# Where the last group's gathers stand on GpSimd's queue: behind the first key stack's ones, ahead of the queries' parting and the other fills

## The chip, the cores and the metric

The kernel runs on one core of one Trainium2 chip. Its metric is the device time of one execution in microseconds, the median of several runs; three runs of the kernel before gave 740.69, 741.37 and 742.08 us. The engines are called by these names: TensorE (PE, and PEld for its weight loads), VectorE (DVE), ScalarE (ACT), GpSimd (POOL), and SyncE (SP), which only issues transfers. ScalarE and GpSimd issue transfers too.

## The reference

Two layers over 16 batches of 112 tokens with 256 features, and a context of 375 rows for each batch. Cut to what matters:

```python
x = x + L0_xattn(layernorm(x), ctx, mask)       # one head, softmax over 375 keys, output normalized
# L0_ffn: top 2 of 8 experts, each token's two expert rows weighted and added
weights, indices = top_k(softmax(xh @ gate_w + gate_b), 2)
routed = sum(weights[..., None] * take_along_axis(out_of_experts, indices))
x = x + shared_experts(xh) + routed
# L1_xattn: 16 heads of 16 features, no mask
q, k, v = split_heads(layernorm(x) @ Wq.T), split_heads(ctx @ Wk.T), split_heads(ctx @ Wv.T)
x = x + merge(softmax(q @ k.T * 0.25) @ v) @ Wo.T
x = x + layernorm(x) @ W.T + b + (layernorm(x) @ V_r) @ C.T
```

## The kernel before

Five streams of instructions, one per engine, are written out by hand and meet at semaphores: `wait_ge(s[name], value)` holds an engine, `then_inc` counts up. Each engine works strictly in its own order. Nothing is scheduled by a program; where a call stands in the function of an engine is where it runs.

The tokens are treated in four groups of four batches (`NG = 4`, `G = 4`). The expert stage works through 35 tiles of 128 routed rows. Each tile's result `y` is written to the array `yscr` in device memory by GpSimd (L1480, semaphores `y_out0` and `y_out1`). When all tiles that hold rows of a group are written, `gather` (L1840 to L1848) fetches for each batch j of the group the two expert rows of every token: two indirect transfers of 112 rows by 256 floats into `yg[:, j, k, :]`, `i` being the group. It first waits for `y_out0` and `y_out1`, and for `mixed`, which says that VectorE has combined the former content of the buffer. Groups 0 to 2 are gathered within the expert stage, four transfers in a row, twice each (`gpsimd_beside`). Group 3 needs the last tile, and so its eight gathers stand in the second layer (`gpsimd`, L1863 on). Their rows are scaled by ScalarE beside batches 2 and 3 (`scaled`, L2155) and added by GpSimd (`combine`).

The second layer begins with a prelude, in which TensorE projects the last six contexts to values (`late_values`, L2283), group 2's queries (L2238), and the scores of batches 0 and 1 (`scores`, L2309). The latter are only for the maxima of each head (L1966, VectorE). A batch's maxima are split into three bf16 parts (`parted`, L1754 to L1766, by VectorE for batches 0 and 1, by GpSimd from batch 2 on), turned by TensorE (`maxima_T`, L2314), copied by VectorE (L1972) and laid into the query stack `qst` by three small transfers on SP (`maxima`, L1787, semaphore `mrow_in`). Then follow 16 batches b. In each TensorE computes the transposed scores in four quads of heads and three chunks of keys (`transposed`, L2329), ScalarE takes the exponential (L2166, semaphore `p_ready`), TensorE multiplies with the values (L2338), and beside that computes the scores of batch b + 2.

The fills on GpSimd, and who needs them: `ones_below(b)` (L1731) writes the lower 32 rows of key stack b, which TensorE needs in batch b; the column of ones in `va` (L1875) is needed from batch 10 on; `zeros_below(1)` (L1735) is needed before SP lays batch 4's maxima into the second query stack. `split_queries` and `split_rest` (L1738 to L1752) part group 2's queries into three bf16 parts in four steps; their end, `q3_ready`, releases ScalarE's store of them (L2089), which stands on ScalarE's stream ahead of batch 0's exponentials.

Of the kernel before, what the change touches and what calls it, by code (L numbers as in the profile page):

```python
# [19 lines left out]
NKC = K // KC  # L20
KP = (NKC - 1) * KC + P
C = D // P
G = 4
NG = B // G
# [1593 lines left out]
def second_layer(nc, tensors, first, routed, dram, out, x_res, weight1, weight2, slots, mhalf, ps, bank, ident, new_semaphore, pool_semaphore):  # L1618
# [9 lines left out]
    s = {n: new_semaphore("d_" + n) for n in (  # L1628
        "weights_in", "wf_ps", "wf_ready", "identb_ready", "below_ready", "scaled", "added", "mixed", "xh_ready",
        "q_ps", "q1_ready", "q2_ready", "q3_ready", "q_out", "qs_in0", "qs_in1",  # L1630
        "k_in0", "k_in1", "k_in2", "k_in3", "v_in0", "v_in1", "s_ps", "s_max", "m_ready", "mT_ps", "mT_ready", "clear", "ones_ready",
        "mrow_in0", "mrow_in1", "st_ps", "p_ready", "pv_ps", "outT_ready", "out_ps", "heads_ready", "o_ps", "x3_ready", "bf_added",
        "f_ps", "fl_ps", "bl_added", "res_ready", "res_out")}
# [13 lines left out]
    EARLY = NG - 1  # L1647
# [82 lines left out]
    def ones_below(pool, b):  # L1730
        pool.memset(kst[b][DEPTH:P, :, :].rearrange("p h t -> p (h t)").bitcast(F32), TWO_MINUS_ONES).then_inc(s["ones_ready"], 1)  # L1731
        pool.wait_ge(s["ones_ready"], b + 1)

    def zeros_below(pool, slot):
        pool.memset(qst[slot][DEPTH:P, :, :].rearrange("p h t -> p (h t)").bitcast(F32), 0.0).then_inc(s["below_ready"], 1)  # L1735
        pool.wait_ge(s["below_ready"], slot + 1)

    def split_queries(eng, i):  # L1738

        eng.wait_ge(s["q1_ready"], (i + 1) * C)  # L1740
        if i:
            eng.wait_ge(s["q_out"], i * 16)
        eng.tensor_copy(qa[:, 1, :, :], qr[:]).then_inc(s["q2_ready"], 1)
        eng.wait_ge(s["q2_ready"], 3 * i + 1)
        eng.tensor_tensor(qr[:], qr[:], qa[:, 1, :, :], ALU.subtract).then_inc(s["q2_ready"], 1)

    def split_rest(eng, i):
        eng.wait_ge(s["q2_ready"], 3 * i + 2)
        eng.tensor_copy(qa[:, 2, :, :], qr[:]).then_inc(s["q2_ready"], 1)
        eng.wait_ge(s["q2_ready"], 3 * i + 3)  # L1750
        eng.tensor_tensor(qa[:, 0, :, :], qr[:], qa[:, 2, :, :], ALU.subtract).then_inc(s["q3_ready"], 1)
        eng.wait_ge(s["q3_ready"], i + 1)  # L1752

    def parted(eng, b):  # L1754

        base, slot = b * 4, b % 2
        eng.wait_ge(s["s_max"], b * 8 + 8)
        if b >= 2:
            eng.wait_ge(s["mT_ps"], b - 1)
        eng.tensor_copy(mparts[:, slot, 0, :], mxh[:, slot, :]).then_inc(s["m_ready"], 1)  # L1760
        eng.wait_ge(s["m_ready"], base + 1)
        eng.tensor_tensor(mr[:, slot, :], mxh[:, slot, :], mparts[:, slot, 0, :], ALU.subtract).then_inc(s["m_ready"], 1)
        eng.wait_ge(s["m_ready"], base + 2)
        eng.tensor_copy(mparts[:, slot, 1, :], mr[:, slot, :]).then_inc(s["m_ready"], 1)
        eng.wait_ge(s["m_ready"], base + 3)
        eng.tensor_tensor(mparts[:, slot, 2, :], mr[:, slot, :], mparts[:, slot, 1, :], ALU.subtract).then_inc(s["m_ready"], 1)  # L1766
# [60 lines left out]
    def rstd_of(pool, n, norm, js=slice(0, G)):  # L1827
        pool.wait_ge(s["mv_ready"], MV + norm + 1)
        pool.tensor_scalar(rstd[:, js], mv[:, js, 1], EPS, None, ALU.add).then_inc(s["pool"], 1)
        pool.wait_ge(s["pool"], n())  # L1830
        pool.tensor_tensor(rstd[:, js], rstd[:, js], mhalf[:, js], ALU.pow).then_inc(s["rstd_ready"], 1)

    def normalized_beside(pool, i, norm):

        pool.wait_ge(s["rstd_ready"], MV + norm + 1)
        for j in range(G):
            pool.tensor_scalar(xh[:, j, :], x_res[:, i * G + j, :], mv[:, j, 0:1], rstd[:, j:j + 1],
                               ALU.subtract, ALU.mult).then_inc(s["xh_ready"], 1)

    def gather(pool, i, j):  # L1840
        b = i * G + j
        for q in range(2):
            pool.wait_ge(routed[f"y_out{q}"], (DONE[i] + 1 - q) // 2 * 16)
        if i:
            pool.wait_ge(s["mixed"], 2 * (b - G + 1))
        for k in range(2):
            pool.indirect_dma_start(out=yg[:, j, k, :], out_offset=None, in_=yscr[0:DONE[i] * P, :],  # L1847
                                    in_offset=bass.IndirectOffsetOnAxis(ap=slots[0:S, k, b:b + 1], axis=0)).then_inc(s[f"y_in{j}"], 16)  # L1848
# [13 lines left out]
    def gpsimd(pool, n):  # L1862

        def combine(i, js):
            for j in js:
                for k in range(2):
                    pool.wait_ge(s["scaled"], 2 * j + k + 1)
                    if k:
                        pool.wait_ge(s["added"], 2 * j + k)
                    pool.tensor_tensor(x_res[:, i * G + j, :], x_res[:, i * G + j, :], yg[:, j, k, :], ALU.add).then_inc(s["added"], 1)  # L1870

        ones_below(pool, 1)
        ones_below(pool, 2)
        ones_below(pool, 3)
        pool.memset(va[:, :, :, :, HD:HD + 1], 1.0).then_inc(s["va_ready"], 1)  # L1875
        pool.wait_ge(s["va_ready"], 2)
        zeros_below(pool, 1)
        pool.wait_ge(s["m_ready"], 4)
        split_queries(pool, EARLY - 1)
        split_rest(pool, EARLY - 1)  # L1880
        i = NG - 1
        for j in range(G):
            if j % 2:
                parted(pool, j // 2 + 2)
            pool.wait_ge(s["p_ready"], (2 * j + 2) * NKC)
            gather(pool, i, j)
        for j in range(0, G, 2):
            combine(i, range(j, j + 2))
            parted(pool, j // 2 + 4)
        rstd_of(pool, n, NORMS["q", i])  # L1890
        normalized_beside(pool, i, NORMS["q", i])
        parted(pool, 6)
        parted(pool, 7)
        split_queries(pool, i)
        split_rest(pool, i)
        for i, batches in enumerate(((8,), (9, 10, 11, 12), (13, 14, 15))):
            for b in batches:
                parted(pool, b)
            rstd_of(pool, n, NORMS["f", i])
            normalized_beside(pool, i, NORMS["f", i])  # L1900
            add_bias(pool, i)
        i = NG - 1
        rstd_of(pool, n, NORMS["f", i], AHEAD)
        rstd_of(pool, n, NORMS["f", i] + 1, LAST)
# [360 lines left out]
    def tensor(t):  # L2265
# [219 lines left out]
        def project_one(i, j):  # L2485
# [46 lines left out]
        project_part("f", LAST, wf)  # L2532

    return {"sync": sync, "gpsimd": gpsimd, "vector": vector, "scalar": scalar, "tensor": tensor, "gpsimd_beside": gpsimd_beside,
            "vector_beside": vector_beside, "scalar_beside": scalar_beside, "tensor_beside": tensor_beside}

# [128 lines left out]
```

## Time and profile before

| what | value |
|---|---|
| median of three runs | 741.37 us (740.69 to 742.08) |
| profiled execution, its own time | 743.03 us |
| its span, first to last instruction | 741.2 us |
| TensorE busy | 721.4 us, 97% of the span |
| VectorE, ScalarE, GpSimd busy | 470.0, 309.8, 271.5 us |
| mean granted clock of TensorE | 0.995 |
| first and last gather of group 3 issued | 552.1 and 570.2 us |
| prelude of the second layer, batches 0 to 3 | 520 to 545 us, 545 to about 590 us |

Shares of busy time are averages over the span, and TensorE's busy time is modelled from the starts of its matmuls, so a full TensorE row doesn't say that it never waited. An engine's idle time matters only where it stands on the chain that ended last. A row of a timeline gives the start, the duration, the engine, the line, the operation, how many of it were merged, and in brackets how long the engine sat idle before and what ended that. "remote" or "issue" there means that no releaser was found.

### The profile page before, as it was taken

What the parts mean: (1) busy time and instruction counts of PE and PEld (TensorE: products, weight loads), DVE (VectorE), ACT (ScalarE), POOL (GpSimd) and SP (SyncE); (2) the same over time, 40 slices, a digit from 0 to 9 for tenths busy, and PEclk for the clock granted to TensorE, in tenths of its full rate; (3) what the DMA queues carried; (4) which work ended last, traced back from release to release, by engine and by line L of the source; (5) the groups of instructions that cost most, each with busy time, mean ns of one, the idle gap of its engine ahead of it and who ended that gap; (6) DMA issues with size and microseconds to landing.
All of it is one profiled execution on the core that took longest, in us unless ns stands there. A gap on an engine that the chain in (4) does not pass through costs nothing.

```text
span 741.2 us, 15552 instructions
## 1 busy us (share of the span) xinstructions
PE 721.4 (97%) x5770; PEld 557.5 (75%) x5770; DVE 470.0 (63%) x1070; ACT 309.8 (42%) x556; POOL 271.5 (37%) x320
## 2 busy tenths in 40 slices
PE   8999999999999999999999999999989999999996
PEld 6686668666866575799999999989766667777774
DVE  4778674557365679644444655738667868778725
ACT  1224221522142122255555554544255755565571
POOL 4985324523410625302201415133823435305051
PEclk9999999999999999999999999999999999999999
DMA  9798934631521595723443423445876675754001
GB/s 256 210 301 247 251 120 155 198 116 42 178 79 53 180 373 182 268 61 99 113 135 95 129 66 105 135 122 160 229 216 188 174 196 170 205 142 129 28 3 50
DMA packets 73517, 114.10 MB, mean 154 GB/s; under 512 B 15154, under 2 KB 59795, under 8 KB 71523
## 3 DMA queue, kind: packets, MB, share of 16 engines
q1 hardware_dynamic: 61856, 85.81, 40.2%
q0 software_dynamic: 6160, 15.67, 6.7%
q10 hardware_dynamic: 5426, 11.63, 5.5%
q8 instruction: 47, 0.77, 0.5%
q14 instruction: 28, 0.22, 0.1%
HBM read 84.27 MB, written 28.41 MB: 152 GB/s over the span
## 4 chain that ended last, share of the span: by engine, by line
PE 86%; DVE 3%; ACT 3%; POOL 2%; issue 2%; DMA 2%; another core or an unknown queue 1%; ACTq 0%; SPq 0%; DVEq 0%
PE ps L1587 17%; PE ps L1204 12%; PE ps L1596 8%; PE ps L1224 6%; PE ps L2338 5%; PE ps L2309 5%; PE ps L1243 5%; PE ps L2329 4%; PE ps L1255 3%; PE ps L1172 3%; PE ps L2302 3%; PE ps L1144 2%; PE ps L2283 2%; PE ps L1179 2%; PE ps L2238 2%
## 5 line engine op out<-in xcount | busy, mean ns | idle before, releaser
L1966 DVE TENSOR_REDUCE mxh<-ps 112x2 f32<-112x750 f32 x128 | 115.2, 932 | 33.8 <-PE ps L2309 30.4
L1587 PE MATMUL ps<-rowsT,w 128*128 128x128 f32 x1120 | 130.8, 275 | 0.0
L1587 PEld LDWEIGHTS ps<-rowsT,w 128*128 128x128 f32 x1120 | 128.0, 192 | 0.1
L2166 ACT ACTIVATE d_pT<-ps 125x448 f32<-125x448 f32 x192 | 91.9, 550 | 46.0 <-PE ps L2329 41.6
L1541 ACT ACTIVATE w<-rw 128x1024 f32 x70 | 73.8, 1055 | 68.8 <-PE ps L1587 50.0
L1204 PE MATMUL ps<-x1T,sw 128*128 128x448 f32 x256 | 101.3, 540 | 0.0
L1204 PEld LDWEIGHTS ps<-x1T,sw 128*128 128x128 f32 x256 | 47.5, 190 | 38.6 <-issue 36.0
L1480 POOL DMA_DIRECT2D yscr<-y x35 | 19.7, 563 | 151.4 <-DVE y L1514 151.4
L1596 PE MATMUL ps<-rw,h 128*128 x280 | 66.4, 380 | 0.0
L2309 PE MATMUL ps<-kst,qst 96*112 96x375 bf16 x256 | 58.8, 334 | 1.6 <-DVE mxh L1966 1.5
L995 ACT ACTIVATE silu<-ps,sb 128x448 f32<-128x448 f32 x32 | 20.3, 633 | 87.0 <-PE ps L1204 78.9
L2329 PE MATMUL ps<-qst,kst 128*128 128x112 bf16 x768 | 53.2, 214 | 2.9 <-ACT d_pT L2166 1.8
L1596 PEld LDWEIGHTS ps<-rw,h 128*128 128x128 f32 x280 | 50.7, 190 | 6.8 <-issue 1.4
L2329 PEld LDWEIGHTS ps<-qst,kst 128*128 128x128 bf16 x768 | 43.2, 99 | 14.4 <-issue 6.0
L1224 PE MATMUL ps<-sw,gluT 128*128 128x256 f32 x224 | 50.7, 379 | 0.0
L1499 DVE TENSOR_TENSOR h<-ps,rb 128x512 f32<-128x512 f32 x35 | 24.1, 689 | 37.1 <-PE ps L1587 31.0
L1224 PEld LDWEIGHTS ps<-sw,gluT 128*128 128x128 f32 x224 | 42.1, 190 | 6.8 <-issue 0.7
L1503 DVE TENSOR_TENSOR h<-ps,rb 128x512 f32<-128x512 f32 x35 | 24.1, 690 | 34.0 <-PE ps L1587 26.7
L388 POOL DMA_INDIRECT xg<-xh_moe,places x32 | 31.5, 985 | 26.0 <-PE ps L1204 18.0
L1847 POOL DMA_INDIRECT yg<-yscr,slots x32 | 32.5, 1016 | 23.1 <-ACT d_pT L2166 13.3
L558 DVE SCALAR_TENSOR_TENSOR gluT<-ps,sb,silu 128x448 f32<-128x448 f32 x32 | 21.8, 681 | 28.5 <-ACT silu L995 27.6
L2309 PEld LDWEIGHTS ps<-kst,qst 96*112 96x112 bf16 x256 | 24.9, 130 | 15.0 <-issue 5.5
(263 smaller groups left out, 1201.1 us busy)
## 6 DMA issues: line engine op xcount, KB each, us to landing
kst<-kscr SPq DMA_DIRECT2D x39, 378.0 KB, 5.1
rw<-in_rw SPq DMA_DIRECT2D x24, 512.0 KB
kscr<-ka SPq DMA_DIRECT2D x16, 567.0 KB
cT<-in_ctx_t SPq DMA_DIRECT2D x17, 378.0 KB, 4.8
ctxT<-in_ctx_t SPq DMA_DIRECT2D x16, 378.0 KB
ctxn<-in_ctx SPq DMA_DIRECT2D x16, 336.0 KB
rows<-xg SPq DMA_DIRECT2D x35, 128.0 KB
rb<-in_rb SPq DMA_DIRECT2D x35, 128.0 KB
```

The costliest lines, as they stand in the source:

```text
L1204: last = mm(bank[up_in(i, m)[k]][:, 0:GS], (sw1, sw2)[k][:, e, c, h * P:(h + 1) * P], x1T[:, c, :], start=c == 0, stop=c == C - 1)
L1224: last = mm(bank[down_in(i, j)][:, 0:D], gluT[:, m, j * P:(j + 1) * P], sw3[:, e, h, :], start=m == 0, stop=m == U - 1)
L1243: last = mm(ps[:, 2 + m, 0:KP], wk1[:, c, m * P:(m + 1) * P], context_T(b)[:, c, :], start=c == 0, stop=c == C - 1)
L1541: A(w12[:, k, :, :], (rw1, rw2)[k][:, e, :, :], ACT.Copy).then_inc(s[("w1_ready", "w2_ready")[k]], 1)
L1587: last = mm(bank[1 + 2 * q + k][:, block], w12[:, k, c, block], rowsT[:, q, c * P:(c + 1) * P], start=c == 0, stop=c == C - 1)
L1596: last = mm(y_bank(n)[:, 0:D], h2[:, q, m * P:(m + 1) * P], rw3[:, e, m, :], start=m == 0, stop=m == HM - 1)
L1847: pool.indirect_dma_start(out=yg[:, j, k, :], out_offset=None, in_=yscr[0:DONE[i] * P, :], in_offset=bass.IndirectOffsetOnAxis(ap=slots[0: ...
L1966: V.tensor_reduce(mxh[:, b % 2, 2 * g:2 * g + 2], ps[0:S, p:p + 2, 0:K], axis=AX_X, op=ALU.max).then_inc(s["s_max"], 1)
L2166: A(pT[:, q % 2, k, :], bank[4 + k][0:KC, 0:QUAD * S], ACT.Exp).then_inc(s["p_ready"], 1)
L2309: last = mm(pair_bank(("score", b, g), k)[0:S, 0:K], qst[i % 2][0:DEPTH, h, j * S:(j + 1) * S], kst[b % 4][0:DEPTH, h, 0:K], start=True, s ...
L2329: last = mm(bank[4 + k][:, h * S:(h + 1) * S], kst[b % 4][:, QUAD * q + h, k * KC:k * KC + P], qst[i % 2][:, QUAD * q + h, j * S:(j + 1) * ...
L2338: last = mm(bank[7][32 * h:32 * h + HD + 1, q * S:(q + 1) * S], values[:, k, QUAD * q + h, :], pT[:, q % 2, k, h * S:(h + 1) * S], start=k ...
```

## The change

GpSimd's stream at the start of the second layer is reordered. All eight gathers of group 3 stand right behind `ones_below(1)`. The parting of group 2's queries follows, then the fills of key stacks 2 and 3, of `va` and of the second query stack, then the partings of the maxima of batches 2 and 3, which stood between the gathers. The waits for `p_ready` ahead of each batch's pair of gathers are gone. The waits inside `gather` remain. No instruction that computes or transfers is added or removed, and no other engine's stream changes.

```diff
--- before.py
+++ after.py
@@ -1869,21 +1869,20 @@
                         pool.wait_ge(s["added"], 2 * j + k)
                     pool.tensor_tensor(x_res[:, i * G + j, :], x_res[:, i * G + j, :], yg[:, j, k, :], ALU.add).then_inc(s["added"], 1)
 
+        i = NG - 1
         ones_below(pool, 1)
+        for j in range(G):
+            gather(pool, i, j)
+        pool.wait_ge(s["m_ready"], 4)
+        split_queries(pool, EARLY - 1)
+        split_rest(pool, EARLY - 1)
         ones_below(pool, 2)
         ones_below(pool, 3)
         pool.memset(va[:, :, :, :, HD:HD + 1], 1.0).then_inc(s["va_ready"], 1)
         pool.wait_ge(s["va_ready"], 2)
         zeros_below(pool, 1)
-        pool.wait_ge(s["m_ready"], 4)
-        split_queries(pool, EARLY - 1)
-        split_rest(pool, EARLY - 1)
-        i = NG - 1
-        for j in range(G):
-            if j % 2:
-                parted(pool, j // 2 + 2)
-            pool.wait_ge(s["p_ready"], (2 * j + 2) * NKC)
-            gather(pool, i, j)
+        parted(pool, 2)
+        parted(pool, 3)
         for j in range(0, G, 2):
             combine(i, range(j, j + 2))
             parted(pool, j // 2 + 4)
```

GpSimd's stream at the end of the expert stage, before. Each row is the line, the operation, the tiles and their shape, and what it waits for; `yscr<-y` is the write of an expert tile, `yg<-yscr,slots` a gather.

```order
L1480 DMA yscr<-y 128x256 [waits c_y_ready] x2
L1731 MEMSET kst 32x3024
L1731 MEMSET kst 32x3024 [waits d_ones_ready] x2
L1875 MEMSET d_va 125x288 [waits d_ones_ready]
L1735 MEMSET qst 32x3584 [waits va_ready]
L1743 CAST qa<-qr 128x896 [waits d_q1_ready,d_q_out,d_m_ready,d_below_ready]
L1745 TENSOR_TENSOR qr<-qr,qa 128x896 [waits d_q2_ready]
L1749 CAST qa<-qr 128x896 [waits d_q2_ready]
L1751 TENSOR_TENSOR qa<-qr,qa 128x896 [waits d_q2_ready]
L1847 DMA yg<-yscr,slots 112x256 [waits c_y_out1,c_y_out0,d_mixed,d_p_ready,d_q3_ready]
L1847 DMA yg<-yscr,slots 112x256
```

And the same place with the change:

```order
L1480 DMA yscr<-y 128x256 [waits c_y_ready] x2
L1731 MEMSET kst 32x3024
L1847 DMA yg<-yscr,slots 112x256 [waits c_y_out1,d_mixed,c_y_out0,d_ones_ready]
L1847 DMA yg<-yscr,slots 112x256
L1847 DMA yg<-yscr,slots 112x256 [waits d_mixed,c_y_out1,c_y_out0]
L1847 DMA yg<-yscr,slots 112x256
L1847 DMA yg<-yscr,slots 112x256 [waits d_mixed,c_y_out1,c_y_out0]
L1847 DMA yg<-yscr,slots 112x256
L1847 DMA yg<-yscr,slots 112x256 [waits d_mixed,c_y_out1,c_y_out0]
L1847 DMA yg<-yscr,slots 112x256
L1743 CAST qa<-qr 128x896 [waits d_q_out,d_q1_ready,d_m_ready]
L1745 TENSOR_TENSOR qr<-qr,qa 128x896 [waits d_q2_ready]
```

Eight gathers now stand where the other fills stood, and no wait for `d_p_ready` is among them; what they still wait for is the last tiles (`c_y_out0`, `c_y_out1`) and the buffers (`d_mixed`).

Where batches 0 to 3 run, GpSimd's stream before, from the parting of batch 2's maxima on:

```order
L1760 CAST mparts<-mxh 112x16 [waits d_mT_ps,d_s_max]
L1762 TENSOR_TENSOR mr<-mxh,mparts 112x16 [waits d_m_ready]
L1764 CAST mparts<-mr 112x16 [waits d_m_ready]
L1766 TENSOR_TENSOR mparts<-mr,mparts 112x16 [waits d_m_ready]
L1847 DMA yg<-yscr,slots 112x256 [waits c_y_out1,d_mixed,c_y_out0,d_p_ready]
L1847 DMA yg<-yscr,slots 112x256
L1847 DMA yg<-yscr,slots 112x256 [waits c_y_out1,d_mixed,c_y_out0,d_p_ready]
L1847 DMA yg<-yscr,slots 112x256
L1760 CAST mparts<-mxh 112x16 [waits d_mT_ps,d_s_max]
```

And with the change, from the third step of the queries' parting to the first of batch 2's maxima:

```order
L1749 CAST qa<-qr 128x896 [waits d_q2_ready]
L1751 TENSOR_TENSOR qa<-qr,qa 128x896 [waits d_q2_ready]
L1731 MEMSET kst 32x3024 [waits d_q3_ready]
L1731 MEMSET kst 32x3024 [waits d_ones_ready]
L1881 MEMSET d_va 125x288 [waits d_ones_ready]
L1735 MEMSET qst 32x3584 [waits va_ready]
L1760 CAST mparts<-mxh 112x16 [waits d_mT_ps,d_s_max,d_below_ready]
L1762 TENSOR_TENSOR mr<-mxh,mparts 112x16 [waits d_m_ready]
L1764 CAST mparts<-mr 112x16 [waits d_m_ready]
```

The gathers between the partings of the maxima are gone, and the fills stand between the queries' parting and that of batch 2's maxima.

## Rows read from the trace of the kernel before

**Rows 1.** The page's chain that ended last, share of the span by engine.
```profile
PE 86%; DVE 3%; ACT 3%; POOL 2%; issue 2%; DMA 2%; another core or an unknown queue 1%; ACTq 0%; SPq 0%; DVEq 0%
```

**Rows 2.** PE's timeline (start us, us, engine, line, operation, count [idle before]), turnings.
```profile
558.79 0.23 PE L2314 MATMUL ps<-identb,mparts 112*48 112x112 bf16 x1
...
571.09 0.23 PE L2314 MATMUL ps<-identb,mparts 112*48 112x112 bf16 x1
...
627.24 0.23 PE L2314 MATMUL ps<-identb,mparts 112*48 112x112 bf16 x1
...
636.25 0.23 PE L2314 MATMUL ps<-identb,mparts 112*48 112x112 bf16 x1
```

**Rows 3.** POOL's timeline, 521 to 563 us.
```profile
521.77 7.95 POOL L1731 MEMSET kst<- 32x3024 f32 x3
...
534.64 0.93 POOL L1743 CAST qa<-qr 128x896 bf16<-128x896 f32 x1 [1.11 <-DVE mparts L1766]
...
538.61 1.89 POOL L1751 TENSOR_TENSOR qa<-qr,qa 128x896 bf16<-128x896 f32 x1
...
552.10 1.02 POOL L1847 DMA_INDIRECT yg<-yscr,slots  x1 [11.61 <-ACT d_pT L2166]
...
562.42 0.93 POOL L1847 DMA_INDIRECT yg<-yscr,slots  x1 [1.69 <-ACT d_pT L2166]
```

**Rows 4.** PE's and ScalarE's timelines in batches 0 and 1, and ScalarE's in batch 7.
```profile
554.83 0.37 PE L2329 MATMUL ps<-qst,kst 128*128 128x112 bf16 x4 [0.96 <-issue]
...
554.23 0.54 ACT L2166 ACTIVATE d_pT<-ps 125x448 f32<-125x448 f32 x1 [2.03 <-PE ps L2329]
...
565.30 1.85 ACT L2166 ACTIVATE d_pT<-ps 125x448 f32<-125x448 f32 x4 [2.27 <-remote]
...
629.69 1.42 ACT L2166 ACTIVATE d_pT<-ps 125x448 f32<-125x448 f32 x3 [0.90 <-PE ps L2329]
```

**Rows 5.** Windows: busy time of five engines, PEclk, DMA share, GB/s.
```profile
567.00:571.00 4.00, 4.00 (x44) 2.81 (x44) 2.12 (x3) 1.65 (x5) 2.60 (x6) 0.57 0.88 254
```

**Rows 6.** Timelines of PE, ScalarE and POOL in the expert stage.
```profile
447.53 3.74 PE L1587 MATMUL ps<-rowsT,w 128*128 128x128 f32 x32
...
453.05 3.74 PE L1587 MATMUL ps<-rowsT,w 128*128 128x128 f32 x32
...
453.53 1.06 ACT L1541 ACTIVATE w<-rw 128x1024 f32 x1 [2.35 <-remote]
...
451.50 0.93 POOL L1847 DMA_INDIRECT yg<-yscr,slots  x1 [0.30 <-issue]
```

**Rows 7.** Timelines of PE and VectorE, 531 to 546 us.
```profile
531.37 0.81 PE L2309 MATMUL ps<-kst,qst 96*112 96x375 bf16 x4
...
534.33 0.17 DVE L1766 TENSOR_TENSOR mparts<-mr,mparts 112x16 bf16<-112x16 f32 x1
...
535.34 0.23 PE L2314 MATMUL ps<-identb,mparts 112*48 112x112 bf16 x1
...
545.31 0.56 PE L2329 MATMUL ps<-qst,kst 128*128 128x112 bf16 x8
```

**Rows 8.** Windows; DMA queues over 552:566, 526:538, 552:553; values; issues on SP and ScalarE.
```profile
532.00:536.00 4.00, 4.00 (x21) 3.17 (x20) 2.76 (x8) 1.31 (x4) 2.80 (x3) 1.00 0.41 105
...
q0 software_dynamic: 261, 0.65, 16.5%
...
q0 software_dynamic: 2, 0.00, 0.1%
...
q8 instruction: 1, 0.02, 7.8%
...
vt<-vscr SPq DMA_DIRECT2D x1, 408.0 KB, 7.2
...
537.77 0.58 SPq L1779 DMA_DIRECT2D vt<-vscr  x1
...
545.52 0.38 ACTq L2089 DMA_DIRECT2D qscr<-qa  x1
```

## The prediction

> **What bounds the kernel now.** I read the page's chain first: TensorE holds 86% of the path that ends last, so anything off TensorE counts only where TensorE stands for it [rows 1]. Then I laid the timelines of POOL, PE, ScalarE and VectorE side by side around the moved work, 520 to 575 us. The stretch has two parts with different limits. From 520 to 545 TensorE works through the late values (projections of the last six contexts) and the first scores without a gap. From 545 the batches of attention begin, in which TensorE and ScalarE wait for each other every half microsecond (scores, exponential, product).
>
> The yardstick is one batch, from one turning of the maxima (L2314) to the next. A batch with nothing beside it takes 636.25 - 627.24 = 9.0 us; batch 1 takes 571.09 - 558.79 = 12.3 us [rows 2], 3.3 us too much. POOL issues two of the eight gathers in batch 0 at 552.10 and two more in batch 1 at 562.42 [rows 3]. Right there something odd stands: ScalarE sits idle 2.03 us before the exponential at 554.23 and 2.27 us before that at 565.30, though TensorE's matmuls for them are recorded as long done; in the undisturbed batch such a wait is 0.90 us [rows 4]. The first costs TensorE 0.96 us (before 554.83). The second is followed by a drop of TensorE's granted clock: 0.57 over 567 to 571, that is, 1.2 GHz for 3.4 of 4 us, half of which, 1.7 us, is lost [rows 5].
>
> The same sign stands in the expert stage beside a burst of four gathers that ends at 452.43: ScalarE waits 2.35 us until 453.53 on an unnamed releaser. But there TensorE loses nothing: its tiles start at 447.53 and 453.05, 5.52 us apart, and the burst lies in between [rows 6]. I read this so: beside gathers, TensorE's signals reach the other engines up to about 2 us late, while it goes on computing. It costs time only where TensorE soon needs the answer. Batches 0 and 1 are such a place, the expert stage is not.
>
> **The change, part by part.** Eight gathers go from batches 0 to 3 to behind the first memset. Before the partings of queries stood three more fills (two key stacks' ones, the column of ones in va, the query stack's zeros); they go behind. Two waits are dropped: p_ready ahead of each pair, and nothing takes its place, because `mixed`, which frees the buffers yg, was complete in the expert stage.
>
> *Gain in batch 1.* 12.3 - 9.0 = **3.3 us**, of which 1.7 is the clock and 1.6 the late signal.
>
> *Gain in batch 0.* The 0.96 us for which TensorE stood: **1.0 us**. I count no more, though VectorE was late too, since its work there has slack. Batches 2 and 3 keep their extra work on ScalarE (the scaling of the gathered rows), and the fourth pair cost nothing that I can separate.
>
> *When the gathers run now.* POOL is free of the first memset at 521.77 + 2.65 = 524.4. The gathers also need the last tile's y in memory; the software queue, which carries it, still moves packets up to 526 and just 2 after that [rows 8]. So they start at about 526.5. One takes 0.93 to 1.3 us and stands 0.3 us behind the last [rows 3, 6], eight take 10 to 11 us: until 537.5. The parting of the queries takes 538.61 + 1.89 - 534.64 = 5.9 us and ends at 543.4 instead of 540.5. Who waits for it is ScalarE, whose store of the queries is issued at 545.52, ahead of all exponentials [rows 8]: 2.1 us are left, so this counts as nothing. If the cover goes, every further microsecond on POOL is one on the path. The four other fills lasted from 524.4 to 534.64 - 1.11 = 533.5, 9.1 us [rows 3], and then end near 552.5. The next thing that is waited for on POOL, the parting of batch 2's maxima, comes when batch 0 is at its end, behind 554.83 [rows 4]; stack 2's ones are due in batch 2, the zeros in batch 4. Nothing.
>
> *Cost: late signals in the new place.* Here TensorE runs ahead of VectorE by a pair of scores. The tightest loop: scores at 531.37, VectorE's maxima and four partings, the last of them at 534.33 + 0.17 = 534.5, TensorE's turning at 535.34 [rows 7]: 0.84 us of slack. A signal 2.1 us late costs 1.3 there; in most other places the slack is larger. With eight gathers in a row I expect one or two late spells. Ends: nothing, and 2 x 1.3 = 2.6. I take **0.6 us**, near the expert stage's zero, because most of the time here goes into value projections that wait for nothing recent.
>
> *Cost: traffic.* Six gathers took 16.5% of 14 us of all DMA engines, 2.3 us; eight are 3.1 us. Around 532 to 536 the engines are busy for only 0.41 of the time: 2.4 us are free [rows 8]. The remaining 0.7 us pushes what follows: the queries of group 1, the rows of maxima of batch 0 (three small transfers on SP's queue), and the values of batch 1, issued last at 537.77 and landed 7.2 us later, 544.97. The maxima stand ahead of them in the queue and TensorE needs them at 545.31 [rows 7, 8]. The slack is thus 0.3 us at least. Ends: nothing, and 3.1 - 0.3 = 2.8. I take **0.7 us**, the backlog uncovered. Batch 4's keys, which shared the engines with the gathers, now land sooner, but nobody waited for them.
>
> The Trainium skill (DMA: Bandwidth & Descriptors, SWDGE vs HWDGE vs iDMA) says that an engine takes turns between its internal queues and switches only at packets; this speaks against the change, because the context of batch 15 (issued 534.80) would then share turns with the gathers and the large rows of the queries. By that rule the sum's traffic term would lie in its upper half, above 1.4. No row here separates it from plain load.
>
> **Sum**: 3.3 + 1.0 - 0.6 - 0.7 = 3.0 us. On the profiled execution, whose span is 741.2 and own time 743.03, that gives 738.2 and 740.0. The profiled execution is 1.7 us above the median of the runs, 741.37, so I put the difference on the median: **738.4 us**. A measurement of this kernel tells about 0.2%, 1.5 us, from no change: under 739.9 is faster, over 742.9 slower. Own range of this case: with both costs at nothing 741.37 - 4.3 = 737.1, and the three runs lie 0.7 about their median, so 736.4 to 739.9.
>
> **Rivals.**
>
> *The clock's part does not come back* (chance 0.18). The profiled execution is slower than the median by the same 1.7 us that the clock costs; timed runs may not have the drop at all, or it comes after a stall elsewhere. Against it: the drop stands in the one execution I see, right behind the late spell of batch 1, and the expert stage's spells had none. Time: 741.37 - 3.0 + 1.7 = 740.1, between faster and same.
>
> *The same loss in a new place* (0.15). The prelude has TensorE without gaps, so each microsecond lost there is lost wholly: two spells on the tight loop (2.6) and traffic near its middle (1.7) eat 4.3. For it: the chain in that stretch is TensorE throughout. Against: expert tiles at 5.52 us in spite of the spell. Time: 741.4.
>
> *Slower: the spells are not the gathers' doing* (0.09). At 552 to 553 the only packet in flight is one of instructions, 16 KB [rows 8]; if TensorE's late signal is its own program arriving late, it stays in batch 0 and 1, with its clock drop, and the gathers only bring traffic where the maxima of batch 0 have 0.3 us to spare. It decides once the backlog passes that. Price up to 2.8, as bounded above, with 0 gained: 741.4 + 2.2 = 743.6 at three quarters of the bound. Against it: the wait at 565.30 has gathers beside it, and so has the one at 453.53.
>
> The Trainium skill (Runtime: NRT & Kernel Launch, Instruction fetch mechanics) calls the cost of crossing a block of instructions mostly hidden, which would speak against this rival; the packet in the row beside a 2 us wait leaves it open for batch 0.
>
> *The gathers wait in vain for something* so that the change does not do what it says: the y of the last tile gates them to 526.5, which is in the sum already. Were they to end 3 us later still, the store at 545.52 would slip by 0.9; I give this no chance of its own.
>
> **How the numbers follow.** Forecast 0.58, rivals 0.18, 0.15, 0.09. Faster: 0.58 + half of 0.18 = 0.67. Same: the other half + 0.15 = 0.24. Slower: 0.09. The range reaches from 736.4 over the first two rivals to 741.8 and leaves out the slower one and the ends of both costs together.
>
> **What would show it.** Right: eight POOL gathers in a row between 526 and 538; batch 1 at about 9.0 us between its turnings; no half clock at 567; ScalarE's waits in batches 0 and 1 under 1 us; a wait of 2 us by ScalarE or VectorE between 528 and 540 that moves TensorE by under 1 us; the first transposed scores at 545.3 to 546.6. Wrong: batch 1 still over 11 us, or a gap of TensorE before L2314 at 535 or before the first L2329, released by VectorE or a DMA, of over 2 us; ScalarE's query store later than 546 with POOL as releaser.

## The result and the profile after

The change makes the kernel **slower by 0.37%**. The median is 744.88 us (740.19 to 747.17, 19 runs) against 741.54 us of before (19 runs) on the same chip, and the ratio is 1.0037 with a 95% interval of 1.0025 to 1.0048. The ratio comes to 2.7 us and the two medians stand 3.3 us apart, where I had forecast 3.0 us less. Two far slower executions, one of 924 us in the eighth experiment and one of 2596 us of the kernel before on the same chip, are left out of the ratios, though not of the medians.

The profiled execution of after is a mild one: its own time is 743.77 us, its span 742.0 us, and it stands only 0.8 us over before's span of 741.2. It lies 1.1 us under its kernel's median, and before's profiled execution 1.5 us over its own. A median's worth of loss isn't in it, so the sizes below are read from the experiments too. The chain still lies on TensorE, as in [rows 1]; the profile page of after has:

```profile
PE 87%; DVE 3%; POOL 2%; ACT 2%; DMA 2%; issue 1%; another core or an unknown queue 1%; ACTq 0%; SPq 0%; DVEq 0%
```

TensorE's timeline of after, the turnings of the maxima (L2313 now; the columns are those of [rows 2]):

```profile
536.70 0.23 PE L2313 MATMUL ps<-identb,mparts 112*48 112x112 bf16 x1
...
552.15 0.23 PE L2313 MATMUL ps<-identb,mparts 112*48 112x112 bf16 x1 [1.71 <-DVE ps L2023]
...
562.80 0.23 PE L2313 MATMUL ps<-identb,mparts 112*48 112x112 bf16 x1
...
571.81 0.23 PE L2313 MATMUL ps<-identb,mparts 112*48 112x112 bf16 x1
```

Take the differences. Batch 1 took 571.81 - 562.80 = 9.0 us, where before had 12.3 [rows 2]: that forecast came true, 3.3 us. Batch 0 took 10.65 us; before, its turnings stood at 547.59 and 558.79, 11.20 apart, so 0.55 us came back there. But the piece ahead of them, from the first turning to the second, took 552.15 - 536.70 = 15.45 us, where before had 547.59 - 535.34 = 12.25 [rows 7]. That is 3.2 us lost, as much as batch 1 gave back. The first turning is 1.36 us late already, by a wait in the expert stage, which the change doesn't touch; the four differences add up to 0.7 of the 0.8 us. TensorE's timeline of after, 408 to 424 us, shows that wait:

```profile
419.09 2.05 PE L1587 MATMUL ps<-rowsT,w 128*128 128x128 f32 x16 [1.48 <-ACT w L1541]
```

ScalarE itself had sat idle until 417.98 us on an unnamed releaser, for 3.47 us, beside a burst of gathers. It is a late signal of the kind that I had read in [rows 6], and here it costs TensorE 1.48 us in the stage in which I had taken the cost for nothing.

What happened between 536.70 and 552.15? GpSimd's timeline of after:

```profile
529.64 1.02 POOL L1847 DMA_INDIRECT yg<-yscr,slots  x1 [3.89 <-DMA yscr<-y]
...
538.42 0.94 POOL L1847 DMA_INDIRECT yg<-yscr,slots  x1 [0.30 <-issue]
539.40 0.93 POOL L1743 CAST qa<-qr 128x896 bf16<-128x896 f32 x1
...
543.37 1.88 POOL L1751 TENSOR_TENSOR qa<-qr,qa 128x896 bf16<-128x896 f32 x1
545.31 5.28 POOL L1731 MEMSET kst<- 32x3024 f32 x2
550.65 0.61 POOL L1881 MEMSET d_va<- 125x288 f32 x1
551.32 3.08 POOL L1735 MEMSET qst<- 32x3584 f32 x1
```

The eight gathers run in a row to 539.36, the parting of the queries to 545.25, and the four fills from 545.31 to 554.40. Now VectorE's timeline in the same microseconds, after:

```profile
539.79 0.21 DVE L1971 COPY mT<-ps 48x112 bf16<-48x112 bf16 x1 [3.92 <-remote]
...
549.41 1.21 DVE L1760 CAST mparts<-mxh 112x16 bf16<-112x16 f32 x1
550.66 0.17 DVE L1762 TENSOR_TENSOR mr<-mxh,mparts 112x16 f32<-112x16 f32 x1
550.87 0.42 DVE L1764 CAST mparts<-mr 112x16 bf16<-112x16 f32 x1
551.33 0.18 DVE L1766 TENSOR_TENSOR mparts<-mr,mparts 112x16 bf16<-112x16 f32 x1
```

and in before (VectorE, and TensorE's second turning):

```profile
546.14 0.17 DVE L1760 CAST mparts<-mxh 112x16 bf16<-112x16 f32 x1
546.35 0.18 DVE L1762 TENSOR_TENSOR mr<-mxh,mparts 112x16 f32<-112x16 f32 x1
546.56 0.17 DVE L1764 CAST mparts<-mr 112x16 bf16<-112x16 f32 x1
...
547.59 0.23 PE L2314 MATMUL ps<-identb,mparts 112*48 112x112 bf16 x1 [0.70 <-DVE ps L2024]
```

The same cast of 112 x 16 elements takes 0.17 us in before and 1.21 us in after. Its end tells why: 549.41 + 1.21 = 550.62, and the two stack fills end at 545.31 + 5.28 = 550.59. The second cast ends at 551.29, and the fill of `va` at 551.26. Both times VectorE's cast ends 0.03 us behind GpSimd's fill. Nothing in the semaphores ties the two together, and a long duration isn't shown as a wait: an instruction that has started and stands still counts as busy. The two subtractions between the casts keep their 0.17 and 0.18 us. The last row of before shows that there was no slack for this: TensorE already waited 0.70 us there for VectorE (L2024 clears a buffer right behind the parting), and now waits 1.71.

Windows of after, 545 to 575 us (columns as in [rows 5]):

```profile
545.00:555.00 10.00, 8.00 (x61) 5.59 (x62) 8.93 (x14) 5.25 (x11) 9.17 (x5) 0.87 0.92 242
555.00:565.00 10.00, 10.00 (x188) 7.10 (x181) 7.98 (x12) 6.10 (x13) 0.83 (x4) 0.96 0.45 116
```

The half clock didn't go away, it moved from batch 1 into batch 0: 0.13 x 10 + 0.04 x 10 = 1.7 us of lost clock, which is 3.4 us at 1.2 GHz, right behind TensorE's stand of 1.71 us.

There is a second loss in this profile: VectorE's copy at 539.79 sat 3.92 us on an unnamed releaser, though TensorE's turning for it is at 536.70, and TensorE in turn stood 1.20 us:

```profile
540.05 1.13 PE L2282 MATMUL ps<-d_wv,cT 128*125 128x256 f32 x4 [1.20 <-DVE mT L1971]
```

That is the late signal which I had bounded at 1.3 us for one spell. Of the 3.2 us lost between the two turnings of this profile, the late signal is thus 1.2, the casts' hold 1.0 (1.71 against 0.70); the rest is not taken apart here.

### The profile page after: what moved, and what is told of

Same layout as the page of the kernel before. It is cut to its first block, busy times and chain, and to the rows that moved or that the text cites. A ratio compares the mean times of both kernels' runs of the same rounds, so it can differ in the third digit from the quotient of the medians.

```text
span 742.0 us, 15548 instructions
## 1 busy us (share of the span) xinstructions
PE 721.9 (97%) x5770; PEld 558.3 (75%) x5770; DVE 469.7 (63%) x1070; ACT 309.3 (42%) x556; POOL 271.2 (37%) x320
## 4 chain that ended last, share of the span: by engine, by line
PE 87%; DVE 3%; POOL 2%; ACT 2%; DMA 2%; issue 1%; another core or an unknown queue 1%; ACTq 0%; SPq 0%; DVEq 0%
PE ps L1587 17%; PE ps L1204 12%; PE ps L1596 8%; PE ps L1224 6%; PE ps L2337 6%; PE ps L2308 5%; PE ps L1243 5%; PE ps L2328 4%; PE ps L1255 3%; PE ps L1172 3%; PE ps L2301 2%; PE ps L1144 2%; PE ps L1179 2%; DVE mxh L1965 2%; PE ps L2237 2%; PE ps L2282 1%
```

## The experiments

Two theories stood against each other. **The fill theory**: VectorE's cast waits for GpSimd's running fill, and the fills were moved onto the parting of batch 1's maxima. **The gather theory**: gathers beside TensorE's gapless prelude cost it, by late signals and by traffic. The kernel before took 738.04, 738.10 and 737.81 us on the three chips on which the ten runs were made, so each run is compared by its ratio to before on its own chip; 0.1% is 0.74 us. The expectations of the first four runs give times on the scale of the comparison's chip, some 3.5 us higher, and are read by the difference from before that they name.

### Fills alone

```diff
         ones_below(pool, 1)
-        ones_below(pool, 2)
-        ones_below(pool, 3)
-        pool.memset(va[:, :, :, :, HD:HD + 1], 1.0).then_inc(s["va_ready"], 1)
-        pool.wait_ge(s["va_ready"], 2)
-        zeros_below(pool, 1)
         pool.wait_ge(s["m_ready"], 4)
         split_queries(pool, EARLY - 1)
         split_rest(pool, EARLY - 1)
+        ones_below(pool, 2)
+        ones_below(pool, 3)
+        pool.memset(va[:, :, :, :, HD:HD + 1], 1.0).then_inc(s["va_ready"], 1)
+        pool.wait_ge(s["va_ready"], 2)
+        zeros_below(pool, 1)
```

> The kernel before, with only the four other fills moved behind the parting of the queries; the gathers stay in batches 0 to 3. Theory F (the fills now run beside VectorE's parting of batch 1's maxima, slow its first step from 0.17 to about 1.2 us, TensorE stands at the turning and its clock halves): 1 to 3 us over the kernel before, 742.5 to 744.5, with that step at about 1.2 us. Theory L (the row of eight gathers makes TensorE's signals late where its turning needs them): as before, 741.5, since the gathers are where they were; batch 1 still about 12.3 us.

Measured: 743.32 us, ratio 1.0075 (1.0062 to 1.0088). The half of the change that I had counted as nothing costs 5.3 us when it is made alone. The fill theory had the side right and the size too small: it expected 1 to 3 us over before and a step of 1.2 us. Timelines of VectorE, GpSimd and TensorE, and the window of batch 0's start:

```profile
546.03 2.90 DVE L1764 CAST mparts<-mr 112x16 bf16<-112x16 f32 x1
...
545.82 3.08 POOL L1735 MEMSET qst<- 32x3584 f32 x1
...
549.78 0.29 PE L2314 MATMUL ps<-identb,mparts 112*48 112x112 bf16 x1 [3.65 <-DVE ps L2024]
...
545.00:555.00 10.00, 6.35 (x62) 4.16 (x60) 8.01 (x11) 3.85 (x10) 3.78 (x3) 0.69 0.43 130
```

The cast meets the zeros' fill here, starts 0.21 us behind it and ends at 548.93, 0.03 us behind its end at 548.90. The first cast, 0.40 us long, ends at 545.79, the fill of `va` at 545.75. TensorE, which has 0.70 us to wait in this place in before, waits 3.65 us, and then gets half clock for about 3.1 / 0.5 = 6.2 of the 10 us.

### Gathers alone

```diff
-        for j in range(G):
-            if j % 2:
-                parted(pool, j // 2 + 2)
-            pool.wait_ge(s["p_ready"], (2 * j + 2) * NKC)
-            gather(pool, i, j)
+        for j in range(G):
+            gather(pool, i, j)
+        parted(pool, 2)
+        parted(pool, 3)
```

This is the kernel before with its fills in their old place; the eight gathers follow the queries' parting in a row.

> The kernel before, with the eight gathers in a row right behind the parting of the queries (from about 541 to 551) and the fills where they were. Theory L: a late spell of 2 to 4 us now ends at about 551, in batch 0 where TensorE and ScalarE wait for each other: batch 0 longer by 2 to 4 us, a half clock behind it, batch 1 at 9.0 us: 741 to 744. Theory F: no fill beside VectorE's parting, and the loss of batch 1 gone: 738 to 739. Theory T (the gathers' traffic pushes the rows of maxima): 738 to 739 too, as the transfers before batch 0 are not disturbed.

Measured: 738.37 us, ratio 1.0006 (0.9995 to 1.0016). The gathers ran from 540.91 to 550.62, the casts took 0.17 and 0.19 us, batch 1 took 9.0 us, and the whole is no different from before. The fill theory had expected the loss of batch 1 to be gained, 2.5 to 3.5 us, the gather theory a late spell in batch 0; neither came. Moving gathers out of batch 1 is worth nothing on this chip. (Batch 0 took 11.3 us in the profile with half clock in it, but that execution, 740.01 us, is the slowest of the eleven.)

### The fills later, behind the last maxima

```diff
+        pool.wait_ge(s["s_max"], 16)
         ones_below(pool, 2)
```

> The changed kernel, with one wait more: GpSimd begins the four other fills only when VectorE has all maxima of batch 1, so that they don't start beside the late part of the prelude but beside the parting's end and batch 0. If theory F holds and the prelude's end is what counts, the turning of batch 1's maxima waits 0.7 us instead of 1.7 and the median falls by 1 to 3 us to 742 to 744; if the fills slow VectorE's small steps wherever they lie beside them, the step stays near 1.2 us and nothing changes, 744.9. Theory L: 744.9, the spell before 539.8 stays.

Measured: 742.09 us, ratio 1.0059 (1.0047 to 1.0072), against 1.0037 and 1.0046 of the change itself: still slow. The mark was badly chosen. The sixteenth maximum is what the four-step parting starts from too, so VectorE and GpSimd started together:

```profile
546.18 2.34 DVE L1764 CAST mparts<-mr 112x16 bf16<-112x16 f32 x1
...
545.84 5.31 POOL L1731 MEMSET kst<- 32x3024 f32 x2 [3.37 <-DVE mxh L1966]
```

The first cast (at 545.76, 0.17 us) was ahead of the fill and wasn't held; the second came 0.34 us behind its start and ended at 548.52, when the first of the two fills was over (545.84 + 2.65 = 548.5). So which cast is held is only a matter of which engine came first.

### Plain transfers instead of gathers

The changed kernel, in which group 3's rows come by plain transfers instead of indirect ones; the last group then adds expert rows that are not its tokens'.

```diff
-            pool.indirect_dma_start(out=yg[:, j, k, :], out_offset=None, in_=yscr[0:DONE[i] * P, :],
-                                    in_offset=bass.IndirectOffsetOnAxis(ap=slots[0:S, k, b:b + 1], axis=0)).then_inc(s[f"y_in{j}"], 16)
+            if i == NG - 1:
+                pool.dma_start(yg[:, j, k, :], yscr[(2 * j + k) * P:(2 * j + k) * P + S, :]).then_inc(s[f"y_in{j}"], 16)
+            else:
...
```

> The changed kernel, with the last group's eight gathers replaced by plain transfers of the same size from fixed rows (the last group's expert rows are thus not the right ones). Theory L, with the address work of the indirect transfers as the cause: VectorE's wait of 3.9 us before the copy of the turned maxima falls to about 1.1, no half clock in the prelude or batch 0, 738 to 740. Theory T (traffic): as the changed kernel, 744 to 745. Theory F: a loss of 1 to 3 us stays, 741 to 743.

Measured: 743.5 us, ratio 1.0069 (1.0054 to 1.0084). The loss doesn't hang on the gathers being indirect. Here again a cast met the zeros' fill:

```profile
547.37 2.40 DVE L1760 CAST mparts<-mxh 112x16 bf16<-112x16 f32 x1
...
546.66 3.08 POOL L1735 MEMSET qst<- 32x3584 f32 x1
...
548.12 0.55 PE L2331 MATMUL ps<-qst,kst 128*128 128x112 bf16 x8 [1.42 <-DMA qst<-mT]
```

The cast ends at 549.77, the fill at 549.74. The last row is a second, smaller loss: batch 0's maxima land late in the query stack, and TensorE waits 1.42 us for them. The 5.1 us are more than the fill theory's 1 to 3; what of them the plain transfers cost is not taken apart.

### The changed kernel again, on another chip

> The changed kernel as it is, a control beside the next three on the same chip. Theory P (VectorE's casts of batch 1's maxima can't run beside a fill of GpSimd and wait for the running fill's end): 2.5 to 5.5 us over the kernel before. In its profile a cast of 112 by 16 that takes 0.17 us elsewhere ends within 0.1 us of a fill's end.

The change as it is, with nothing edited. Measured: 742.06 us, ratio 1.0046 (1.0033 to 1.0059). Timelines of VectorE and TensorE, and the window:

```profile
545.70 2.62 DVE L1760 CAST mparts<-mxh 112x16 bf16<-112x16 f32 x1
...
549.84 0.29 PE L2313 MATMUL ps<-identb,mparts 112*48 112x112 bf16 x1 [2.71 <-DVE ps L2023]
...
545.00:555.00 10.00, 6.59 (x68) 4.66 (x68) 8.06 (x11) 4.26 (x10) 6.92 (x4) 0.68 0.64 186
```

The stack fills lie from 543.00 to 548.28, the cast ends at 548.32. The profiled execution, 742.31 us, is near the median, so this is the better picture of the changed kernel: a stand of 2.71 us, and 3.2 us of clock lost in the window. In the comparison's own profile the first cast fell nearer to the end of the fills, and took 1.21 us instead of 2.62. No signal came late in this profile, although all eight gathers lie in the prelude.

### The fills behind the parting of batch 1

```diff
+        pool.wait_ge(s["m_ready"], 8)
         ones_below(pool, 2)
```

One wait is added to the changed kernel: the fills start when VectorE's last step of batch 1's parting is done.

> The changed kernel, with a wait on GpSimd that lets the four other fills begin only when VectorE has parted batch 1's maxima (m_ready 8). Theory P: the four steps of the parting take 0.17 us each again, TensorE's wait at the turning falls to 0.5 to 0.7 us, the time falls by 3 to 5 us to that of the kernel before, or a little under it. Theory L (the gathers' place costs): it stays within 1 us of the changed kernel.

Measured: 738.83 us, ratio 1.0006 (0.9994 to 1.0018), 0.4% better than the changed kernel on the same chip, with the gathers exactly where the change puts them. GpSimd, VectorE, TensorE and the window:

```profile
545.48 5.28 POOL L1731 MEMSET kst<- 32x3024 f32 x2 [3.89 <-DVE mparts L1766]
...
544.98 0.17 DVE L1764 CAST mparts<-mr 112x16 bf16<-112x16 f32 x1
...
545.63 0.55 PE L2329 MATMUL ps<-qst,kst 128*128 128x112 bf16 x8 [1.74 <-DMA qst<-mT]
...
545.00:555.00 10.00, 8.91 (x155) 6.39 (x159) 8.11 (x13) 5.79 (x12) 8.94 (x5) 1.00 0.58 164
```

GpSimd idles 3.89 us and the kernel is 3.2 us faster for it. The clock is whole. The wait of 1.74 us for the maxima's rows is new against the profile of before, and yet the time is no different from before.

### Short fills

The changed kernel, each stack fill cut into eight pieces of 378 and 448 columns (the zeros' fill likewise):

```diff
-        pool.memset(kst[b][DEPTH:P, :, :].rearrange("p h t -> p (h t)").bitcast(F32), TWO_MINUS_ONES).then_inc(s["ones_ready"], 1)
+        at = kst[b][DEPTH:P, :, :].rearrange("p h t -> p (h t)").bitcast(F32)
+        step = at.shape[1] // 8
+        for k in range(8):
+            last = pool.memset(at[:, k * step:(k + 1) * step], TWO_MINUS_ONES)
+        last.then_inc(s["ones_ready"], 1)
```

> The changed kernel, with each fill of a key or query stack cut into eight pieces of 0.35 to 0.4 us (the same bytes). Theory P in the form 'a cast waits for the end of the one instruction that runs': the casts take at most 0.6 us, the time falls by 2 to 4 us against the changed kernel. If the cast waits until GpSimd has nothing left to do, or shares its bandwidth throughout, the casts stay at 1 to 3 us and the time with them.

Measured: 739.2 us, ratio 1.0013 (1.0003 to 1.0023). The fills still lie across the parting, and TensorE doesn't wait for VectorE at the second turning; it waits 1.73 us for the maxima's rows, as in the sixth run:

```profile
545.77 0.50 DVE L1772 CAST mparts<-mr 112x16 bf16<-112x16 f32 x1
...
542.14 5.89 POOL L1734 MEMSET kst<- 32x378 f32 x16
```

The first cast took 0.24 us, the second 0.50. One piece lasts 5.89 / 16 = 0.37 us, and a cast now waits for at most that. The length of one GpSimd instruction is what counts, not how much GpSimd does.

### VectorE's casts as operations of two inputs

```diff
-        eng.tensor_copy(mparts[:, slot, 0, :], mxh[:, slot, :]).then_inc(s["m_ready"], 1)
+        if b < 2:
+            eng.tensor_tensor(mparts[:, slot, 0, :], mxh[:, slot, :], mxh[:, slot, :], ALU.max).then_inc(s["m_ready"], 1)
+        else:
+            eng.tensor_copy(mparts[:, slot, 0, :], mxh[:, slot, :]).then_inc(s["m_ready"], 1)
```

and the same for the second cast, in the changed kernel. The maximum of a tile with itself, rounded to bf16, is the cast.

> The changed kernel, with VectorE's two casts of each parting (batches 0 and 1) written as the maximum of the tile with itself, an instruction with two inputs and the same result. The subtractions between them, with two inputs, took 0.18 us beside a fill. Theory P, held to casts alone: all four steps at 0.17 to 0.2 us though the fills run beside them, the time falls by 3 to 5 us against the changed kernel, to the kernel before or under it. If any small instruction of VectorE can be held up by a fill: one of them takes 1 to 3 us and the time stays.

Measured: 739.41 us, ratio 1.0014 (1.0001 to 1.0027): 2.7 us under the changed kernel on the same chip (2.9 without the execution of 924 us), a little less than the 3 to 5 expected. VectorE beside the stack fills, which run from 543.60 to 548.88:

```profile
546.14 0.17 DVE L1761 TENSOR_TENSOR mparts<-mxh 112x16 bf16<-112x16 f32 x1
546.35 0.18 DVE L1765 TENSOR_TENSOR mr<-mxh,mparts 112x16 f32<-112x16 f32 x1
546.56 0.17 DVE L1768 TENSOR_TENSOR mparts<-mr 112x16 bf16<-112x16 f32 x1
546.77 0.17 DVE L1772 TENSOR_TENSOR mparts<-mr,mparts 112x16 bf16<-112x16 f32 x1
...
543.60 5.28 POOL L1731 MEMSET kst<- 32x3024 f32 x2
```

Same place, same fill, same elements and types: only the kind of operation differs, and the hold is gone. It is thus neither the engine nor the memory as such that waits, but the cast with one source. That its source lies in SBUF seems to belong to it. In after, VectorE's copy of the turned maxima, one source too but read from PSUM (the `ps` of the rows), falls into the zeros' fill (551.32 to 554.40) and keeps its length:

```profile
553.63 0.20 DVE L1971 COPY mT<-ps 48x112 bf16<-48x112 bf16 x1
```

What is left over before, 0.1%, goes with a wait of TensorE of 2.06 us for the maxima's rows and half clock behind it in the profile.

### Fills alone, without casts

The kernel of the first experiment with VectorE's partings as in the last one.

> The kernel before with only the four fills moved behind the queries' parting (that alone cost 5.3 us), and VectorE's two casts in each of its four-step partings of batches 0 and 1 written as maximum of the tile with itself. No gather is moved. Theory: the whole of the 5.3 us is VectorE's cast standing for the running fill, and what follows from that. Then the steps take 0.17 to 0.2 us beside the fill, TensorE waits for VectorE under 0.8 us at the turning of batch 1, and the time is 737.5 to 739.5, within 0.15% of before. Rival: the fills cost in a second way too (GpSimd's parting of batch 2 comes later, or the first gathers do): then 1 us or more stays, 739.5 to 742.

Measured: 738.06 us, ratio 1.0004 (0.9993 to 1.0016), where the first experiment had 1.0075. The four fills in their new place cost 0.75% with casts beside them and nothing that shows without. This closes the books on that half of the change. On these chips it answers the other half too, since the gathers stand here in batches 0 and 1 as in before, from 552.05 to 562.72. The turnings of TensorE (L2320 here) and a gather between them:

```profile
557.29 0.23 PE L2320 MATMUL ps<-identb,mparts 112*48 112x112 bf16 x1
...
560.55 0.93 POOL L1853 DMA_INDIRECT yg<-yscr,slots  x1 [1.41 <-ACT d_pT L2172]
...
566.30 0.23 PE L2320 MATMUL ps<-identb,mparts 112*48 112x112 bf16 x1
```

Batch 1 takes 9.0 us with two gathers in it, where the profile of the comparison's before had 12.3, and the first run's batch 1 takes 9.0 us too. The window shows the start of batch 0 as it is undisturbed:

```profile
545.00:555.00 10.00, 8.93 (x141) 5.92 (x140) 8.97 (x16) 6.43 (x14) 6.46 (x5) 1.00 0.56 162
```

### Four gathers in front, four behind

The changed kernel with two batches' gathers ahead of the queries' parting, two behind, and the fills behind the parting of batch 1:

```diff
-        for j in range(G):
+        for j in range(2):
             gather(pool, i, j)
...
         split_rest(pool, EARLY - 1)
+        for j in range(2, G):
+            gather(pool, i, j)
+        pool.wait_ge(s["m_ready"], 8)
         ones_below(pool, 2)
```

> The changed kernel with four gathers ahead of the queries' parting and four behind it, and the four fills waiting for the last step of VectorE's parting of batch 1 (m_ready at 8). Theory: the gathers' place costs only by its traffic, which makes batch 0's rows of maxima land late (TensorE waited 1.4 to 2.1 us for them with eight in front). With four in front the wait falls under 1 us, and batches 0 and 1 keep their short intervals (under 10.2 and 9.1 us): 736.5 to 738, 0.1 to 0.2% under before. Rival: what the gathers cost batches 0 and 1 is not saved by any place, since another wait in them takes over: within 0.1% of before, 737.5 to 739.

Measured: 737.49 us, ratio 0.9997 (0.9988 to 1.0006). The wait for the maxima's rows is gone, as TensorE's timeline shows:

```profile
544.93 0.55 PE L2331 MATMUL ps<-qst,kst 128*128 128x112 bf16 x8
...
547.10 0.23 PE L2316 MATMUL ps<-identb,mparts 112*48 112x112 bf16 x1 [0.70 <-DVE ps L2026]
...
558.41 0.23 PE L2316 MATMUL ps<-identb,mparts 112*48 112x112 bf16 x1
```

But batch 0 takes 558.41 - 547.10 = 11.3 us instead of 9.9 with all eight in front. Yet this execution (739.36 us) is the slowest of its eleven, with half clock for 3.4 us of the window from 545 to 555 (0.83). Its mean clock is 0.995, as in one other of the eleven, and 0.997 or more in the nine left. So the longer batch 0 isn't shown to be what the median pays. It is the best median of the ten, and no different from the kernel before: the gain of 0.1 to 0.2% that I expected isn't there, and none of the orders I tried beats before.

## Why the prediction was wrong

- **The four other fills, "Nothing": this is the step that failed.** I asked of the moved fills only who waits for GpSimd. I didn't ask which engine works beside them in the new place. Their stretch, forecast to about 552.5, holds the parting of batch 1, which stands in before at 546.14. A cast that falls into a fill can wait for up to its 3.08 us, and at the second turning TensorE has no slack against that. I had worked out 0.84 us of slack for the first turning alone, which the fills don't meet. The loss is 3.2 us with all gathers in front (742.06 against 738.83, one chip) and 5.3 us with the gathers in the batches (743.32 against 738.06, two chips with nearly the same before). The first experiment's profile shows the two parts: from the first turning to the second 15.2 us against 12.25 in the ninth, 2.9 us of standing, and batch 0 11.6 against 9.75, 1.9 us more with half clock in it.
- The Trainium skill (SBUF — State Buffer, Who interferes with whom) states what I should have weighed here: VectorE and GpSimd share one pair of ports, a VectorE cast can take a mode that uses it, and whichever instruction comes first keeps it to its end. It adds that a VectorE operation with two inputs collides only with a GpSimd instruction that reads the memory, not with one that only writes. The rows agree where the fill came first: 2.90, 2.62, 2.40 and 2.34 us for a cast beside a fill, 0.17 and 0.18 us for the operation with two inputs beside fills, which only write. No run here shows a fill that a cast holds.
- **Gain in batch 1, 3.3 us**: the interval fell from 12.3 to 9.0 us as forecast. **Gain in batch 0, 1.0 us**: 0.55. But the gain was not one of the kernel, and this is the second step that failed. With the gathers moved and nothing else, the time is the same (1.0006), and with the whole change but for the fills beside the parting too (1.0006). With gathers in batch 1 it takes 9.0 us in the first and ninth runs' profiles. I had read a loss in a single profile as what the gathers cost in every run. On the fifth run's chip the forecast of 3.0 us less met 3.4 more (1.0046): about 3.4 us of the miss are the gain that isn't there (1.0006), 3.0 the fills. What the gathers cost the kernel before on the comparison's chip stays open, since neither half was run there alone.
- **The half clock**: of 1.7 us, forecast to vanish. In the profiles of the changed kernel it stands in batch 0 instead, once or twice as long. The five profiles in which TensorE stood 1.5 us or more for VectorE at the second turning (after and the first, third, fourth and fifth run) lost 1.7 to 3.4 us of clock behind that; of the six other runs three lost none and three 1.7. The drop went with that stand each time, but it came without one too, and the stands of 1.74 and 1.73 us for the maxima's rows in the sixth and seventh run had none behind them. What else it hangs on stays open. In the comparison, three of the changed kernel's 19 runs took 740.2 to 741.0 us, at a mean granted clock of 0.997 to 0.999; the other 16 took 742.2 to 747.2 us at 0.991 to 0.996. Whether the casts missed the fills in those three isn't shown, as none of them was profiled.
- **Late signals, 0.6 us**: one spell of 1.20 us in the prelude on the comparison's chip, inside the bound, and none on the others. The reason I gave for a small cost, that TensorE loses nothing to them in the expert stage, didn't hold: it lost 1.48 us there in after, by gathers which the change doesn't move.
- **Traffic, 0.7 us, bound 2.8**: it delayed just what I named, the rows of the maxima, by 1.42 to 2.06 us of waiting TensorE in four profiles. In the third and fifth run it waits 1.08 and 0.70 us in the same place, put down to ScalarE and to a fill for key stack 2, which batch 0 doesn't need. So the mechanism was right and the size two to three times what I took, within the bound; in the sixth run's median the wait doesn't show.
- **The queries' parting, end at 543.4**: it ended at 545.25, since the gathers began at 529.64 and not at 526.5: 1.4 us of that is the late start from the expert stage, the rest the y of the last tile. ScalarE's store went out at 548.79 us, 3.5 us behind the parting's end, so it wasn't GpSimd that it waited for. Nothing in these runs prices that apart.
- **Rivals.** The first rival's doubt, that timed runs may not have the drop at all, was well founded on the experiments' chips: of the 66 timed runs of before there, 8 have a mean granted clock of 0.995, that of the profile which the forecast was read from, and the others 0.997 or more. For the comparison's before only the profiled run's clock is on record. The same loss in a new place (0.15) describes the comparison's profile, 3.2 us lost ahead of 3.8 gained, but not its medians. The slower rival had the right side with the wrong mechanism: signals come late beside the gathers in both places on the comparison's chip, and its traffic term alone gives no slower kernel, as the sixth run shows. Small slips of the recorded text change nothing: it says three more fills and names four, and three quarters of 2.8 are 2.1 and not 2.2.

## What to carry to other kernels

When work is moved on an engine that shares something with another, list what the *neighbour* runs in the new place, besides who waits for the moved work. A long fill is harmless in time that nobody else's critical cast falls into. Where it can't be placed there, cut it into short instructions, or write the neighbour's short critical step in a form that isn't held. And a stall seen in one profile of one chip is a candidate for a gain, not a gain: a repetition on another chip would have put the 4.3 us of gain in this forecast in doubt.

## What the runs showed of the hardware

- A VectorE cast of 112 x 16 elements, fp32 to bf16 within SBUF, ended 0.03 or 0.04 us behind the end of a GpSimd fill that had started before it, in five profiles, eight casts in all. Its row shows a longer duration and no idle time. The casts of batch 0 in after (535.07 and 535.49), beside GpSimd's issue of gathers, kept their 0.17 us. Once it was otherwise: in the third run a cast that starts beside a gather's issue (533.16 to 534.09) takes 0.33 us and ends with it. Why just this one isn't shown.

```profile
533.75 0.33 DVE L1764 CAST mparts<-mr 112x16 bf16<-112x16 f32 x1
```

- On the chip of the comparison, both profiles have signals of TensorE that reach the other engines late, all of them beside or just behind a burst of indirect transfers (the first such waits end at 132 us in before and at 208 in after); the ten profiles of the experiments have none, beside the same bursts. The expert stage's exemplar of [rows 6] reads so in the comparison's after and in the sixth run:

```profile
454.80 1.06 ACT L1541 ACTIVATE w<-rw 128x1024 f32 x1 [2.26 <-remote]
```

```profile
453.54 1.06 ACT L1541 ACTIVATE w<-rw 128x1024 f32 x1 [1.49 <-PE ps L1587]
```

  The comparison's results don't name their chip; the kernel before is 3.5 us slower there than on the three chips of the experiments, and the changed one 2.8 us, which sets it apart. Whether the late signals are that difference, and what causes them, stays open: no run was made there besides the comparison.
